# Score copies from PSUM on ScalarE, and row maxima by a reduction on VectorE, in a top-k attention kernel

## The chip, the cores and the metric

The kernel runs on one core of a Trainium2 chip. The metric is the device time of one execution in microseconds: 3460.84 us in the median of three runs, 3460.31 to 3461.46.

## What is computed

For 32 batches of 256 tokens with 256 features: a gated cross attention with 16 heads that keeps the 64 largest scores of a row, then a gated linear layer with operands rounded to an 8-bit float format.

```python
def _topk_attention(Q, K, V, topk):                     # topk = 64, d = 16
    scores = jnp.einsum('bhqd,bhkd->bhqk', Q, K) / jnp.sqrt(jnp.asarray(d, Q.dtype))
    topk_scores, topk_idx = jax.lax.top_k(scores, topk)
    probs = jax.nn.softmax(topk_scores, axis=-1)
    sel = gather(V, topk_idx)
    return jnp.einsum('bhqk,bhqkd->bhqd', probs, sel)

x = x + tanh(g_xattn) * attention(layernorm(x), ctx, ctx)      # projections Wq, Wk, Wv, Wo with biases
x = x + tanh(g_ffn) * fp8_linear(layernorm(x))
```

## The kernel before

The order of every engine is written out by hand, one function for each engine, and semaphores join them. A batch has two **stages**, g = 0 and g = 1, of 8 heads each; stage i = 2b + g. A head has two tiles of 128 query rows by 256 keys (jh = 0, 1), so a stage has 16 score tiles of 128 x 256, and `score_sb` is a ring of four stages. A stage is worked in four **quarters**, r = 0 to 3. While VectorE finishes stage i, four stages are in hand at once:

- Stage i + 2: its scores arrive. PE (`scores`, L615) computes a head into one of the two halves `ps_s[:, n % 2]` of PSUM, each 512 wide, and may go on to head H when H - 1 heads have been copied (`s_copied`). VectorE (`copy_scores`, L966) copies a head in two instructions of 256 elements. They read with a step of 16 elements, since the queries stand in PSUM as (j, t) and in `score_sb` as (t, j), and the same instruction takes the row maximum into `mx`. After the eighth head `start_thresholds` (L977 to L980) makes the first threshold X from the maxima.
- Stage i + 1: its thresholds are searched. In each quarter ScalarE counts 14 tiles against X (`guide_counts`, L796, one ACTIVATE and a read of the accumulator each), VectorE the other two (L988); `update_thresholds` (L1003 to L1041) waits for both and moves X, and its last step (L1021 or L1041) releases the next quarter's counts through `s_thr`.
- Stage i: `final_tiles` masks four tiles a quarter (L1066, L1071) and takes the eight largest of the rest (L1077); `final_thresholds` in the last quarter picks the 64th score. Where a row stays unsure, `settle` at the next stage's first quarter sorts it out.
- Stage i - 1: it is mixed. ScalarE takes the exponentials of a head (`exps`, L806), VectorE masks them (`probs`, L1169), PE transposes them (L626), ScalarE evacuates (`evacuate_probs`, L814), and PE multiplies by the values (L641). Exponentials of head n wait until VectorE has masked head n - 2.

ScalarE's order in a quarter is: counts of the stage ahead, then for heads 2r and 2r + 1 an evacuation (of a head four earlier) and the exponentials. Other work stands between: L775 (projections, behind heads 6 of g = 0 and 0 of g = 1), L766 and L767 (front, behind head 4 of g = 0), L783 (`queries_by_head`, 3.6 us, behind head 5 of g = 1), L821 (mixed values, ahead of heads 0 and 4).

VectorE's order in a quarter is: masks of the finals, two counts, copies of head 2r in two halves around L1071, L1077, masking of one head of probabilities, the update with the masking of a second head and the copies of head 2r + 1 between its steps. In the last quarter the copies of head 2r + 1 and the start of the thresholds stand ahead of the update:

```python
if last and has(1):
    for jh in range(2):
        copy_scores(i + 2, fresh, 2 * r + 1, jh)
    start_thresholds(i + 2, fresh)
steps = update_thresholds(i + 1, ahead, r) if guided else iter(())
```

Ahead of the batches VectorE copies the scores of stages 0 and 1. SP issues the DMAs that turn queries and keys by way of DRAM; GpSimd does layernorms and the splitting of operands. `schedule` writes out four batches at either end and loops over pairs of batches between.

## Time and profile before

| | |
|---|---|
| median of the runs | 3460.84 us |
| the profiled execution: from its first to its last instruction (span) | 3454.8 us |
| VectorE busy | 3099.7 us, 90% |
| ScalarE busy | 2725.2 us, 79% |
| PE busy | 1812.2 us, 52% |
| GpSimd busy | 669.6 us, 19% |
| the chain that ended last | VectorE 54%, ScalarE 18%, issue 18%, PE 6% |

The profile gives no device time of its own for the profiled execution, only its span; the median of the runs lies 6.0 us above it. The chain is followed back from the last instruction, at each step to what released it. "Issue" is time in which an engine waited for nothing that the profile shows. An instruction's row may overlap the next one's on its engine, so the cost of one in a full queue is the distance of the starts.

### The profile page before, as it was taken

The page shows a single profiled execution, that of the slowest core. Times are in us where ns is not written, and L with a number is a line of the kernel's source. Part 1 is how long each engine was busy: PE and PEld are TensorE (multiplying, and loading weights), DVE is VectorE, ACT ScalarE, POOL GpSimd, SP SyncE. Part 2 cuts the span into 40 slices and gives each one's busy share as a digit, 9 for nine tenths or more (in the row PEclk, how much of TensorE's full clock was granted, in tenths as well). Part 3 has the DMA queues.
Part 4 walks back from the last instruction along what each step waited for, and adds up shares of the span by engine and source line. Part 5 has one row for each costly group of instructions (what it writes and reads, how often), then busy time and mean ns, then how long its engine had stood idle before and what let it go on. Part 6 is the DMA issues. An engine that isn't in the chain of part 4 may idle for free.

```text
span 3454.8 us, 50006 instructions
## 1 busy us (share of the span) xinstructions
PE 1812.2 (52%) x6928; PEld 973.4 (28%) x6928; DVE 3099.7 (90%) x13458; ACT 2725.2 (79%) x9158; POOL 669.6 (19%) x914
## 2 busy tenths in 40 slices
PE   4155555555455555455555555555455455554555
PEld 2122232322223323222232233322223222232222
DVE  2798999999999999999989999999999999999995
ACT  3788788878688888787878888788788788887872
POOL 3111121121122121111211212121211112211112
PEclk7577677777777777677777777777677777777767
DMA  5122333322233222332223333222333123332111
GB/s 95 29 32 49 49 53 56 53 40 47 47 49 59 45 44 44 51 53 44 46 43 54 56 52 58 41 42 46 51 57 50 33 45 59 49 59 35 26 23 44
DMA packets 425740, 164.74 MB, mean 48 GB/s; under 512 B 219504, under 2 KB 425328, under 8 KB 425408
## 3 DMA queue, kind: packets, MB, share of 16 engines
q1 hardware_dynamic: 425024, 161.54, 27.4%
q14 instruction: 314, 2.57, 0.3%
q0 software_dynamic: 384, 0.33, 0.1%
q8 instruction: 18, 0.29, 0.0%
HBM read 102.57 MB, written 59.24 MB: 47 GB/s over the span
## 4 chain that ended last, share of the span: by engine, by line
DVE 54%; ACT 18%; issue 18%; PE 6%; DVEq 2%; DMA 1%; POOL 0%; SPq 0%; ACTq 0%; POOLq 0%
ACT act_junk L796 14%; DVE p_sb L1169 8%; DVE masked L1066 6%; DVE masked L1071 5%; DVE score_sb L966 5%; DVE following L1077 4%; DVE dve_junk L988 3%; DVE fbias_sb L1213 2%; DVE A L1013 2%; PE ps_t L626 1%; PE ps_o L641 1%; ACT qs L783 1%; PE ps_a L592 1%; ACT pT_sb L814 1%; DVE X L1021 1%
## 5 line engine op out<-in xcount | busy, mean ns | idle before, releaser
L796 ACT ACTIVATE act_junk<-score_sb,X 128x256 bf16<-128x256 f32 x3584 | 1764.7, 498 | 104.4 <-DVE X L1041 79.1
L626 PE MATMUL ps_t<-ident,p_sb 128*128 128x128 f32 x2048 | 452.7, 362 | 1497.6 <-DVE p_sb L1169 893.8
L806 ACT ACTIVATE e_sb<-score_sb,nmx 128x256 f32<-128x256 f32 x1024 | 466.2, 505 | 516.7 <-DVE p_sb L1169 511.7
L626 PEld LDWEIGHTS ps_t<-ident,p_sb 128*128 128x128 f32 x2048 | 322.3, 187 | 1586.7 <-issue 891.1
L641 PE MATMUL ps_o<-pT_sb,v_aug 128*32 128x256 f32 x2048 | 767.9, 515 | 0.5 <-ACT pT_sb L814 0.5
L796 ACT ACTIVATION_READ_ACCUMULATOR act_junk<-score_sb,X 128x1 f32 x3584 | 684.5, 191 | 0.0
L1169 DVE SCALAR_TENSOR_TENSOR p_sb<-score_sb,thr,e_sb 128x256 f32<-128x256 f32 x1024 | 505.6, 515 | 17.9 <-PE ps_t L626 5.0
L966 DVE TENSOR_SCALAR_CACHE_REDUCE score_sb<-ps_s 128x256 f32<-128x256 f32 x1024 | 416.5, 413 | 50.7 <-PE ps_s L615 50.4
L1066 DVE TENSOR_SCALAR_CACHE_REDUCE masked<-score_sb,X 128x256 f32<-128x256 f32 x1024 | 426.0, 471 | 11.0 <-issue 7.7
L1077 DVE MAX8 following<-masked 128x8 f32<-128x256 f32 x1024 | 357.4, 408 | 1.1 <-DVE masked L1071 0.9
L641 PEld LDWEIGHTS ps_o<-pT_sb,v_aug 128*32 128x32 f32 x2048 | 232.3, 136 | 318.9 <-issue 268.0
L1071 DVE SCALAR_TENSOR_TENSOR masked<-masked,score_sb 128x1024 f32<-128x1024 f32 x256 | 313.3, 1224 | 0.1
L814 ACT COPY pT_sb<-ps_t 128x512 f32<-128x512 f32 x512 | 294.0, 574 | 3.9 <-PE ps_o L641 3.9
L499 POOL CAST split<-proj 128x512 bf16<-128x512 f32 x64 | 42.2, 660 | 1157.6 <-ACT proj L775 980.3
L615 PE MATMUL ps_s<-ks,qs 96*128 96x256 bf16 x1024 | 224.4, 306 | 59.7 <-DVE score_sb L966 45.1
L988 DVE SCALAR_TENSOR_TENSOR dve_junk<-score_sb,X,minus_twos 128x256 bf16<-128x256 f32 x512 | 227.4, 480 | 0.1
L472 POOL TENSOR_SCALAR var<-mv 128x2 f32<-128x2 f32 x64 | 14.2, 222 | 805.4 <-DVE mv L912 802.8
L528 POOL TENSOR_TENSOR ysum_sb<-y_sb,magic_sb 128x512 f32<-128x512 f32 x32 | 44.0, 1374 | 562.1 <-DVE magic_sb L938 562.1
L615 PEld LDWEIGHTS ps_s<-ks,qs 96*128 96x128 bf16 x1024 | 76.6, 103 | 251.3 <-issue 128.2
L783 ACT COPY qs<-q_rows 96x4096 bf16<-96x4096 bf16 x32 | 115.0, 3593 | 12.9 <-DMA q_rows<-q_scr 12.9
L1003 DVE TENSOR_TENSOR X<-aim,count 128x16 f32<-128x16 f32 x256 | 48.1, 188 | 84.9 <-ACT act_junk L796 62.6
L601 PE MATMUL ps_a<-wT,cT 128*128 128x256 f32 x256 | 101.6, 535 | 0.0
(149 smaller groups left out, 3088.0 us busy)
## 6 DMA issues: line engine op xcount, KB each, us to landing
...
o_scr<-o_sb SPq DMA_DIRECT2D x128, 128.0 KB, 2.8
...
```

What stands on the lines that cost most here:

```text
L615: ins = nc.tensor.matmul(ps_s[:, n % 2, jh * TOK:(jh + 1) * TOK], qs[p][:, h, 8 * jh:8 * jh + 8, :].rearrange("d j t -> d (j t)"), ks[p][: ...
L626: ins = nc.tensor.transpose(ps_t[:, n % 2, kc * TOK + jh * P:kc * TOK + jh * P + P], p_sb[:, n % 2, jh, kc * P:kc * P + P], ident[:])
L641: ins = nc.tensor.matmul(ps_o[32 * c:32 * c + 32, half * TOK:(half + 1) * TOK], v_aug[p][:, 2 * h + kc, :], pT_sb[:, n % 2, kc * TOK:(kc + ...
L796: ins = nc.scalar.activation(act_junk[:, t, :], score_sb[:, slot, t, :], ACT.Sign, scale=-1.0, bias=X[slot % 2][:, 0, t:t + 1], accum_out= ...
L806: ins = nc.scalar.activation(e_sb[:, n % 2, jh, :], score_sb[:, slot, t, :], ACT.Exp, bias=nmx[:, slot, t:t + 1])
L814: nc.scalar.copy(pT_sb[:, n % 2, :], ps_t[:, n % 2, :]).then_inc(s_PT, 1)
L966: ins = nc.vector.tensor_scalar(dst, src, 0.0, None, ALU.add, ALU.max, accum_out=mx[:, slot, t:t + 1])
L988: ins = nc.vector.scalar_tensor_tensor(dve_junk[:, t - ACT_TILES, :], score_sb[:, slot, t, :], X[slot % 2][:, 0, t:t + 1], minus_twos[:], ...
L1066: nc.vector.tensor_scalar(masked[:, k, :], score_sb[:, slot, t, :], X[slot % 2][:, 0, t:t + 1], None, ALU.is_gt, ALU.add, accum_out=final_ ...
L1071: nc.vector.scalar_tensor_tensor(masked[:], masked[:], -BIG, scores, ALU.mult, ALU.add).then_inc(s_fin, 1)
L1077: nc.vector.max(following[:, t, 1:], masked[:, k, :]).then_inc(s_fin, 1)
L1169: ins = nc.vector.scalar_tensor_tensor(p_sb[:, n % 2, jh, :], score_sb[:, slot, t, :], thr[:, slot, t:t + 1], e_sb[:, n % 2, jh, :], ALU.i ...
```

## The change

ScalarE copies a head's scores, 128 x 512, from PSUM in one instruction, in the same order of elements. It does so ahead of the evacuation and the exponentials of each of the two heads of a quarter, behind the quarter's counts. The copy waits for the scores, and for the probabilities of the stage whose place in the ring it takes. VectorE takes the maxima of a head with one `tensor_reduce` over 2 x 256 in SBUF; it waits for the copy. Heads 2r and 2r + 1 of a quarter are no longer reduced in the places of their copies: the first quarter has head 0 alone, the next two have two heads each (2r - 1 and 2r), the last has heads 5, 6 and 7. `start_thresholds` waits for the eighth reduction. Ahead of the batches ScalarE makes the 16 copies of stages 0 and 1, behind both calls of `queries_by_head` and ahead of its first counts.

```diff
--- before.py
+++ after.py
@@ -240,6 +240,7 @@
         s_va = sem("values_ready")
         s_S = sem("scores_in_psum")
         s_copied = sem("scores_copied")
+        s_max = sem("maxima_ready")
         s_step = sem("selection_steps")
         s_sel = sem("selected")
         s_exp = sem("exp_done")
@@ -797,6 +798,14 @@
                                                bias=X[slot % 2][:, 0, t:t + 1], accum_out=count[slot % 2][:, t:t + 1])
                 ins.then_inc(s_cnt, 1)
 
+            def copy_scores(i, slot, n):
+
+                H = GH * i + n
+                act.wait_ge(s_S, H + 1)
+                act.wait_ge(s_P, at(H - RING * GH + 1))
+                nc.scalar.copy(score_sb[:, slot, 2 * n:2 * n + 2, :].rearrange("p a (t j) -> p a t j", j=NJ),
+                               ps_s[:, n % 2, :].rearrange("p (a j t) -> p a t j", a=2, t=D)).then_inc(s_copied, 1)
+
             def exps(i, slot, n):
                 H = GH * i + n
                 act.wait_ge(s_sel, i + 1)
@@ -862,6 +871,8 @@
                         if guided:
                             guide_counts(2 * b + g + 1, (2 * p + g + 1) % RING, r)
                         for n in (2 * r, 2 * r + 1):
+                            if has(1):
+                                copy_scores(2 * b + g + 2, (2 * p + g + 2) % RING, n)
                             if mixes:
                                 after_transposes(mb, mp, mg, n, has(-1))
                                 exps(2 * mb + mg, 2 * mp + mg, n)
@@ -880,6 +891,9 @@
                             if has(-3) and (g, n) == (0, 7):
                                 evacuate_ffn(b - 3)
 
+            for i in range(2):
+                for n in range(GH):
+                    copy_scores(i, i, n)
             for r in range(GUIDES):
                 guide_counts(0, 0, r)
             schedule(act, batch)
@@ -955,22 +969,17 @@
             nc.vector.tensor_tensor(kq_sb[:], y_sb[:], magic_sb[:], ALU.add).then_inc(s_kq, 1)
             dve.wait_ge(s_kq, 1)
 
-            def copy_scores(i, slot, n, jh):
-
-                H = GH * i + n
-                if jh == 0:
-                    dve.wait_ge(s_S, H + 1)
-                t = 2 * n + jh
-                src = ps_s[:, n % 2, jh * TOK:(jh + 1) * TOK].rearrange("p (j t) -> p t j", t=D)
-                dst = score_sb[:, slot, t, :].rearrange("p (t j) -> p t j", j=NJ)
-                ins = nc.vector.tensor_scalar(dst, src, 0.0, None, ALU.add, ALU.max, accum_out=mx[:, slot, t:t + 1])
-                if jh == 1:
-                    ins.then_inc(s_copied, 1)
+            def row_maxima(i, slot, n):
+
+                dve.wait_ge(s_copied, GH * i + n + 1)
+                carry(dve)
+                nc.vector.tensor_reduce(mx[:, slot, 2 * n:2 * n + 2], score_sb[:, slot, 2 * n:2 * n + 2, :], AX.X,
+                                        ALU.max).then_inc(s_max, 1)
 
             def start_thresholds(i, slot):
 
                 x = X[slot % 2]
-                dve.wait_ge(s_copied, GH * i + GH)
+                dve.wait_ge(s_max, GH * i + GH)
                 carry(dve)
                 dve.wait_ge(s_thr, at(GUIDES * i))
                 carry(dve)
@@ -1220,8 +1229,7 @@
             front_moments(1)
             for i in range(2):
                 for n in range(GH):
-                    copy_scores(i, i, n, 0)
-                    copy_scores(i, i, n, 1)
+                    row_maxima(i, i, n)
                 if i == 0:
                     start_thresholds(0, 0)
             for r in range(GUIDES):
@@ -1249,13 +1257,11 @@
                             guide_counts(i + 1, ahead, r)
                         if r == 0 and mixes:
                             read_unsure(i - 1)
-                        if has(1):
-                            copy_scores(i + 2, fresh, 2 * r, 0)
                         next(finals)
                         if r == 0 and mixes:
                             convert_unsure(i - 1)
-                        if has(1):
-                            copy_scores(i + 2, fresh, 2 * r, 1)
+                        if has(1) and r:
+                            row_maxima(i + 2, fresh, 2 * r - 1)
                         next(finals, None)
                         if r == 0 and mixes:
                             settle(i - 1, mixed)
@@ -1268,8 +1274,8 @@
                                 probs(of, at_slot, first, jh)
                         last = r == GUIDES - 1
                         if last and has(1):
-                            for jh in range(2):
-                                copy_scores(i + 2, fresh, 2 * r + 1, jh)
+                            for n in (2 * r, 2 * r + 1):
+                                row_maxima(i + 2, fresh, n)
                             start_thresholds(i + 2, fresh)
 
                         steps = update_thresholds(i + 1, ahead, r) if guided else iter(())
@@ -1282,8 +1288,8 @@
                             next(steps, None)
                         for jh in range(2):
                             next(ending, None)
-                            if has(1) and not last:
-                                copy_scores(i + 2, fresh, 2 * r + 1, jh)
+                            if has(1) and not last and jh:
+                                row_maxima(i + 2, fresh, 2 * r)
                             next(steps, None)
                         for _ in ending:
                             next(steps, None)
```

ScalarE from head 5 in the third quarter to the end of the fourth, in a stage g = 1, before. The names are those of the text above; `qs` are the rearranged queries.

```order
L814 COPY pT_sb<-ps_t 128x512
L806 ACTIVATE e_sb<-score_sb,nmx 128x256 x2
L783 COPY qs<-q_rows 96x16x16x16
L796 ACTIVATE act_junk,count<-score_sb,X 128x256 x14
L814 COPY pT_sb<-ps_t 128x512
L806 ACTIVATE e_sb<-score_sb,nmx 128x256 x2
L814 COPY pT_sb<-ps_t 128x512
L806 ACTIVATE e_sb<-score_sb,nmx 128x256 x2
```

The same place in the changed kernel, where L797 are the counts, L806 the new score copy, L815 the exponentials, L823 the evacuation and L784 the queries:

```order
L806 COPY score_sb<-ps_s 128x512
L823 COPY pT_sb<-ps_t 128x512
L815 ACTIVATE e_sb<-score_sb,nmx 128x256 x2
L784 COPY qs<-q_rows 96x16x16x16
L797 ACTIVATE act_junk,count<-score_sb,X 128x256 x14
L806 COPY score_sb<-ps_s 128x512
L823 COPY pT_sb<-ps_t 128x512
L815 ACTIVATE e_sb<-score_sb,nmx 128x256 x2
L806 COPY score_sb<-ps_s 128x512
L823 COPY pT_sb<-ps_t 128x512
L815 ACTIVATE e_sb<-score_sb,nmx 128x256 x2
```

Three copies have come in (that of head 4 stands ahead of this piece, right behind the third quarter's counts), and the last of them, of head 7, stands behind the copy, evacuation and exponentials of head 6.

VectorE in the fourth quarter, before, behind its counts L988 and up to the update L1003:

```order
L966 TENSOR_SCALAR score_sb,mx<-ps_s 128x256
L1071 SCALAR_TENSOR_TENSOR masked<-masked,score_sb 128x1024
L966 TENSOR_SCALAR score_sb,mx<-ps_s 128x256
L1077 MAX following<-masked 128x8 x4
L966 TENSOR_SCALAR score_sb,mx<-ps_s 128x256 x2
L977 TENSOR_SCALAR nmx<-mx 128x16
L978 TENSOR_SCALAR X<-mx 128x16
L979 MEMSET A 128x32
L980 MEMSET B 128x32
L1003 TENSOR_TENSOR X<-aim,count 128x16
```

And in the changed kernel, where L976 is the reduction, L986 to L989 the start of the thresholds and L1012 the update:

```order
L1080 SCALAR_TENSOR_TENSOR masked<-masked,score_sb 128x1024
L976 TENSOR_REDUCE mx<-score_sb 128x2
L1086 MAX following<-masked 128x8 x4
L976 TENSOR_REDUCE mx<-score_sb 128x2 x2
L986 TENSOR_SCALAR nmx<-mx 128x16
L987 TENSOR_SCALAR X<-mx 128x16
L988 MEMSET A 128x32
L989 MEMSET B 128x32
L1012 TENSOR_TENSOR X<-aim,count 128x16
```

Four half-copies have gone, a reduction stands ahead of L1086, and two reductions, of heads 6 and 7, stand where two half-copies stood ahead of the start of the thresholds and the update.

## Rows read from the trace of the kernel before

**Rows 1.** The page, part 1: busy us, share of the span, instructions, by engine.

```profile
PE 1812.2 (52%) x6928; PEld 973.4 (28%) x6928; DVE 3099.7 (90%) x13458; ACT 2725.2 (79%) x9158; POOL 669.6 (19%) x914
```

**Rows 2.** Grouped lines: line, engine, operation, tiles, shapes, count | busy us, mean ns | idle before, releasers.

```profile
L806 ACT ACTIVATE e_sb<-score_sb,nmx 128x256 f32<-128x256 f32 x1024 | 466.2, 505 | 516.7 <-DVE p_sb L1169 511.7 <-DVEq L1161 4.8
...
L966 DVE TENSOR_SCALAR_CACHE_REDUCE score_sb<-ps_s 128x256 f32<-128x256 f32 x1024 | 416.5, 413 | 50.7 <-PE ps_s L615 50.4 <-DVE B L980 0.2
...
L1003 DVE TENSOR_TENSOR X<-aim,count 128x16 f32<-128x16 f32 x256 | 48.1, 188 | 84.9 <-ACT act_junk L796 62.6 <-DVE B L980 21.8 <-issue 0.4
```

**Rows 3.** Timeline of VectorE, stage g = 1: start us, us, instruction [idle before].

```profile
1932.46 0.16 DVE L1003 TENSOR_TENSOR X<-aim,count 128x16 f32<-128x16 f32 x1
...
1955.60 0.41 DVE L966 TENSOR_SCALAR_CACHE_REDUCE score_sb<-ps_s 128x256 f32<-128x256 f32 x1
...
1955.94 0.41 DVE L966 TENSOR_SCALAR_CACHE_REDUCE score_sb<-ps_s 128x256 f32<-128x256 f32 x1
...
1956.71 0.38 DVE L977 TENSOR_SCALAR nmx<-mx 128x16 f32<-128x16 f32 x1 [0.36 <-DVE score_sb L966]
...
1957.61 0.18 DVE L1003 TENSOR_TENSOR X<-aim,count 128x16 f32<-128x16 f32 x1 [0.37 <-DVE B L980]
```

**Rows 4.** Timeline of ScalarE, the same stretch.

```profile
1936.01 0.51 ACT L796 ACTIVATE act_junk<-score_sb,X 128x256 bf16<-128x256 f32 x1 [1.25 <-DVE X L1041]
...
1942.91 0.34 ACT L821 COPY o_sb<-ps_o 128x256 f32<-128x256 f32 x1
...
1949.29 0.51 ACT L796 ACTIVATE act_junk<-score_sb,X 128x256 bf16<-128x256 f32 x1
...
1956.18 0.57 ACT L814 COPY pT_sb<-ps_t 128x512 f32<-128x512 f32 x1
...
1957.45 0.57 ACT L814 COPY pT_sb<-ps_t 128x512 f32<-128x512 f32 x1
```

**Rows 5.** Timelines of VectorE and ScalarE, stage g = 0 of the same batch.

```profile
1985.79 0.16 DVE L1003 TENSOR_TENSOR X<-aim,count 128x16 f32<-128x16 f32 x1
...
1996.15 0.19 ACT L796 ACTIVATION_READ_ACCUMULATOR act_junk<-score_sb,X 128x1 f32 x1
1996.24 0.35 ACT L821 COPY o_sb<-ps_o 128x256 f32<-128x256 f32 x1
...
1996.60 0.18 DVE L1003 TENSOR_TENSOR X<-aim,count 128x16 f32<-128x16 f32 x1 [0.72 <-ACT act_junk L796]
...
2000.47 0.53 ACT L796 ACTIVATE act_junk<-score_sb,X 128x256 bf16<-128x256 f32 x1
...
2007.37 0.58 ACT L814 COPY pT_sb<-ps_t 128x512 f32<-128x512 f32 x1
...
2008.21 0.17 DVE L977 TENSOR_SCALAR nmx<-mx 128x16 f32<-128x16 f32 x1 [0.72 <-DVE score_sb L966]
...
2008.64 0.83 ACT L775 ACTIVATE proj<-ps_a,b_col 128x256 f32<-128x256 f32 x2
2009.35 0.59 ACT L814 COPY pT_sb<-ps_t 128x512 f32<-128x512 f32 x1
...
2008.91 0.18 DVE L1003 TENSOR_TENSOR X<-aim,count 128x16 f32<-128x16 f32 x1 [0.37 <-DVE B L980]
```

**Rows 6.** Grouped lines of the nearest operations.

```profile
L814 ACT COPY pT_sb<-ps_t 128x512 f32<-128x512 f32 x512 | 294.0, 574 | 3.9 <-PE ps_o L641 3.9
...
L821 ACT COPY o_sb<-ps_o 128x256 f32<-128x256 f32 x128 | 44.8, 350 | 14.3 <-PE ps_o L641 14.3
...
L1200 DVE TENSOR_REDUCE rowmax<-yabs_sb 128x2 f32<-128x512 f32 x32 | 21.9, 686 | 1.1
```

**Rows 7.** Timelines of VectorE and ScalarE before the batches begin.

```profile
57.34 0.42 DVE L966 TENSOR_SCALAR_CACHE_REDUCE score_sb<-ps_s 128x256 f32<-128x256 f32 x1 [28.34 <-PE ps_s L615]
...
69.55 3.60 ACT L783 COPY qs<-q_rows 96x4096 bf16<-96x4096 bf16 x1 [12.92 <-DMA q_rows<-q_scr]
...
80.30 0.17 DVE L1003 TENSOR_TENSOR X<-aim,count 128x16 f32<-128x16 f32 x1 [9.14 <-ACT act_junk L796]
```

## The prediction

> **What bounds the kernel now.** I read the page's busy line first: VectorE is busy for 3099.7 us of 3454.8, ScalarE for 2725.2 [rows 1]. VectorE looks like the bound, and a change that takes work from it looks good. The grouped lines correct this. ScalarE's idle time stands almost wholly ahead of the exponentials (516.7 us, of which 511.7 until VectorE's masking of probabilities L1169), and VectorE's update of the thresholds L1003 waits now and then for ScalarE's counts (62.6 us) [rows 2]. So the two engines run in a loop: a threshold X from VectorE starts 14 counts on ScalarE, whose end starts the next update. I therefore take the time from one update (L1003) to another, in two stretches of one batch, and ask in each which engine's own work fills it.
>
> In the stage g = 1, the update of the second quarter starts at 1932.46 and that of the fourth at 1957.61: 25.15 us [rows 3]. ScalarE's rows fill nearly all of it without a wait [rows 4]: X is released 3.55 us after the first of these updates (counts from 1936.01), 14 counts take 6.90 (to 1942.91), the work of heads 4 and 5 and the 3.6 us rearrangement of queries L783 take 6.38 (to 1949.29), the next 14 counts 6.89 (to 1956.18), and the update follows 1.43 later. In the stage g = 0 it is 1985.79 to 2008.91, 23.12 us: 10.45 to the end of the first counts (3.55 and 6.90 again), 4.23, 6.90 and 1.54 [rows 5]. In both, ScalarE is the busy one between the second and the fourth quarter. From a fourth quarter's update to the next second quarter's, VectorE fills the time and ScalarE waits ahead of its exponentials. The two kinds of stretch alternate, and an engine's idle total says nothing about the stretches in which it has none.
>
> **The change part by part.** *What VectorE gives and gets.* A head's two score copies go (starts 0.34 apart, 1955.60 and 1955.94 [rows 3]; so 0.69 a head), and one maximum over 2 x 256 comes. The nearest row is the reduction L1200 over the same 128 x 512, which takes 686 ns [rows 6]; successive rows overlap by 0.07 as the copies' do (413 ns long, 0.34 apart), so 0.62 in a full queue. VectorE's saving is 0.07 us a head, 36 us over 512 heads. Below, a reduction of 1x speed is bounded by 2 x 413 = 826 ns on the one side, and 574 ns (ScalarE's row for 512 elements) on the other; I take 0.69, the same operation on the same shape. The Trainium skill ("VectorE: DVE Perf Modes", section on the TRN2 errata) counts 58 cycles plus one an element from SBUF and 120 from PSUM, at 0.96 GHz. That is an estimate of 594 ns for the reduction and of 392 for each copy, 190 ns saved a head instead of 70; it would take about 0.1 us off each of the 61 exposed reductions below, 6 us in all, and the row decides.
>
> In the first quarter of a stage the two half-copies ahead of the maxima are not replaced there (their head's maximum comes later), which saves 0.69, less 0.07 of overlap that the copy filled. In the second quarter another 0.07 is saved. Where a copy stood between two dependent little steps of the update, two gaps were filled and now one is. A gap is worth something between nothing and the 0.36 that L977 waits for its predecessor [rows 3]; I take 0.13, since L977 also has a second semaphore to pass. Over a first and second quarter that nets to 0.6 us saved a stage, 1.2 a batch, in the stretches where VectorE is the bound. ScalarE's two copies a quarter lie there in its waits ahead of the exponentials.
>
> *What ScalarE gets.* 512 copies of 128 x 512 from PSUM. L814 is such a copy: 574 ns [rows 6], of which 0.10 lies under the next instruction, so 0.48 in the queue (ScalarE's counts overlap by as much: 0.49 apart in rows 4, 6.90 over 14, with an accumulator read behind each). The new one reads PSUM with a step of 16 elements, which no ScalarE row shows; L821 writes in pieces of 16 and takes 350 ns for 256 elements, so 0.70 for 512 is the upper end, 0.57 the lower, and I take 0.57, because VectorE's copies read with just this step and show no price for it. All 512 add 246 us of ScalarE time. In the stretch from second to fourth update none of it is hidden: heads 4 and 5 add 2 x 0.48 = 0.96.
>
> *The new wait.* In the last quarter the maxima of heads 6 **and 7**, and then the start of the next thresholds, stand ahead of the update (order of VectorE, above). Head 7's copy is on ScalarE behind 14 counts, the copy of head 6, the evacuation L814 and the exponentials of head 6, and in g = 0 the evacuation of a projection too (order of ScalarE, above). The update used to wait for the counts alone. From the counts' end: copy 0.48, evacuation and exponentials 1.27 (1956.18 to 1957.45 [rows 4]), copy 0.57, release 0.27 (the counts' last row ends at 1996.34, the update starts at 1996.60 [rows 5]), reduction 0.69, wait for its result 0.42 (0.36 [rows 3] and the queue), start of thresholds 0.70 (2008.21 to 2008.91 [rows 5]; 0.90 in rows 3, where L977 took 0.38): 4.40 in g = 1, and with the projection's 0.71 (2008.64 to 2009.35 [rows 5]) 5.12 in g = 0. Behind this wait on VectorE stand the update, the final thresholds of the stage and the next masks; on ScalarE the exponentials of head 7 wait for those masks, so both engines lose it.
>
> *The sums.* g = 1: 3.61 + 6.90 + (6.38 - 0.08 of a wait that goes + 0.96 = 7.26) + 6.89 + 4.40 = 29.06, against 25.15: +3.91. g = 0: 3.61 + 6.90 + (4.23 + 0.96 = 5.19) + 6.90 + 5.12 = 27.72, against 23.12: +4.60. A batch is +8.5 - 1.2 = +7.3 (3.61 is the 3.55 with 0.06 more for the update: 0.13 of a gap less 0.07 of a reduction). Stages 1 to 61 prepare scores and mix at once, 30.5 batches: +223. Stage 0 has no exponentials on ScalarE: +2.
>
> *Waits for scores.* VectorE waits 50.4 us for PE at its copies, 28.3 of it at the first copy of the program [rows 2, 7]. The other 22 go, because ScalarE comes for those heads only after its counts: -22.
>
> *The prologue.* On ScalarE the first score copies stand behind both rearrangements of queries, and the second of them waits for a DMA until 69.55 and ends at 73.1 [rows 7]. VectorE began copying at 57.34. Now 16 copies follow 73.1. Two heads lie ready; the other 14 go round through PE and two buffers, at no less than ScalarE's 0.48 each and about 0.85 if release, copy and release (0.27, 0.57, 0.27) and PE's part all show; I take 0.75, so until 84.5; counts of 6.9 and the release bring the first update to 91.7 instead of 80.30 [rows 7]: +11.
>
> The sum against the profiled execution is 223 + 2 - 22 + 11 = +214, so a span of 3669. The median of the runs stands 6.0 above that span, so **3675 us**, 6.2% slower.
>
> **The rivals.** *The copies fit into ScalarE's waits* (faster). 246 us of copies against 511.7 us of waiting [rows 2], and PE gets its buffers from an engine that waits anyway. Then VectorE's 0.6 a stage is kept in 61 stages (-37), PE's waits go (-22) and only the prologue is lost (+11): 3413. It decides if head 7's copy has ended when VectorE comes to its maximum, which asks for 2.3 us of slack behind ScalarE's counts in the fourth quarter; the rows show ScalarE going from count to count there. For it speaks only the total. 6%.
>
> *Only the new wait costs* (slower, less). Heads 4 and 5 are copied in time that the rows of other batches leave free: 61 x 0.96 = 59 less, 3616. Against it, L783 and the front evacuations follow without a gap [rows 4, 5]. 8%.
>
> *The strided read is slow on ScalarE* (slower, more). If each of the 16-element steps cost another pass, a copy would take 0.44 us longer. Four copies of a stage stand on the path, 61 x 4 x 0.44 = 107, and the prologue 16 x 0.44 = 7: 3789. VectorE reads the same pattern at 413 ns for 256 elements, which speaks against it. The Trainium skill ("SBUF — State Buffer", on SBUF "cachelines") says that PSUM has lines of 8 bytes and that a non-contiguous access slows matmuls significantly; a step of 64 bytes would be hit by that if it holds for a ScalarE read, and by that rule the time is this rival's. No run here shows it yet. 10%.
>
> *It comes out even* (the prologue and the wait paid by VectorE's savings): nothing in the sums is near; 1%.
>
> **How the numbers follow.** My forecast has 75%; within it the copy may be 0.70 (+31), the reduction 0.62 or 0.83, and the dependent gaps may be absent (-8), so 3620 to 3720. The range takes in the milder rival at 3616 and half of the strided one: 3610 to 3760. A difference of under 0.2% could not be told from none. Faster 0.06, same 0.01, slower 0.93.
>
> **What would show each step.** The copy's row on ScalarE at 0.57 to 0.60 us, the reduction at 0.69. VectorE idle ahead of the reductions until ScalarE's copy, about 3.5 us a stage and some 200 us in all, almost all in fourth quarters. ScalarE's counts in third and fourth quarters start without idle time; its busy time near 2970, VectorE's near 3065. From a second quarter's update to a fourth's: 29.1 in g = 1, 27.7 in g = 0. The first update near 91.7. I am wrong if VectorE's wait at the reductions is under 100 us in all, if the copy takes over 0.7, or if the steps from fourth to second quarter, which should shorten by 0.6, lengthen instead.

## The result, and the profile after

The changed kernel takes 3649.11 us in the median of four runs (3648.31 to 3651.48); the kernel before takes 3460.57 on the same chip. The ratio is 1.0551, with a 95% interval of 1.0538 to 1.0564: slower, inside the predicted range and 26 us under the predicted time.

The page of the changed kernel, its first line of parts 1 and 4, and the grouped lines that answer to rows 1, 2 and 6 (L976 is the reduction, L806 the new copy, L815 the exponentials, L1012 the update):

```profile
PE 1867.2 (51%) x6928; PEld 982.3 (27%) x6928; DVE 3049.9 (84%) x11959; ACT 2967.7 (81%) x9670; POOL 662.9 (18%) x914
...
DVE 38%; ACT 37%; issue 19%; DVEq 2%; PE 2%; DMA 1%; ACTq 1%; POOL 0%; SPq 0%; POOLq 0%
...
L815 ACT ACTIVATE e_sb<-score_sb,nmx 128x256 f32<-128x256 f32 x1024 | 469.0, 511 | 484.5 <-DVE p_sb L1178 480.0
...
L976 DVE TENSOR_REDUCE mx<-score_sb 128x2 f32<-128x512 f32 x512 | 348.2, 682 | 282.9 <-ACT score_sb L806 275.6
...
L806 ACT COPY score_sb<-ps_s 128x512 f32<-128x512 f32 x512 | 294.3, 577 | 3.1 <-PE ps_s L616 3.1
...
L1012 DVE TENSOR_TENSOR X<-aim,count 128x16 f32<-128x16 f32 x256 | 62.9, 246 | 83.5 <-ACT act_junk L797 60.1
```

The copy lasts 577 ns and the reduction 682, as forecast (0.57 and 0.69). VectorE's load fell by 50 us and ScalarE's rose by 243, yet ScalarE's idle time ahead of its exponentials fell by only 32 (516.7 in [rows 2]). That difference hides two larger ones: by the steps from one update to the next, this idle time grew by 121 us in the steps behind a fourth quarter's update (152.8 to 274.2) and fell by 155 in the others. The copies used up idle time in one place, and the new wait made it in another. A wait of 275.6 us is new, ahead of the reductions; 46.1 of it is before the batches, so 229.5 is in the loop. On the chain that ended last ScalarE's share went from 18% to 37%.

VectorE at the end of a fourth quarter of g = 1 (start, us, instruction, idle before it and its releaser; this answers to [rows 3]):

```profile
2077.08 0.69 DVE L976 TENSOR_REDUCE mx<-score_sb 128x2 f32<-128x512 f32 x1 [2.27 <-ACT score_sb L806]
2078.84 0.69 DVE L976 TENSOR_REDUCE mx<-score_sb 128x2 f32<-128x512 f32 x1 [1.08 <-ACT score_sb L806]
2079.87 0.17 DVE L986 TENSOR_SCALAR nmx<-mx 128x16 f32<-128x16 f32 x1 [0.34 <-DVE mx L976]
...
2080.56 0.18 DVE L1012 TENSOR_TENSOR X<-aim,count 128x16 f32<-128x16 f32 x1 [0.37 <-DVE B L989]
```

And ScalarE in the same stretch (to [rows 4]), with the last counts first:

```profile
2075.86 0.51 ACT L797 ACTIVATE act_junk<-score_sb,X 128x256 bf16<-128x256 f32 x1
...
2076.35 0.58 ACT L806 COPY score_sb<-ps_s 128x512 f32<-128x512 f32 x1
2076.82 0.59 ACT L823 COPY pT_sb<-ps_t 128x512 f32<-128x512 f32 x1
2077.29 0.93 ACT L815 ACTIVATE e_sb<-score_sb,nmx 128x256 f32<-128x256 f32 x2
2078.11 0.58 ACT L806 COPY score_sb<-ps_s 128x512 f32<-128x512 f32 x1
```

The row behind the last counts starts at 2076.35, which is taken as the counts' end here as in the prediction, and the update starts at 2080.56, 4.21 us later (4.40 forecast; 1.43 before). In between stands exactly the forecast chain: copy of head 6, evacuation and exponentials, copy of head 7, reduction, start of the thresholds. In g = 0 the two waits are 2.28 and 1.80 and the update starts 5.16 after the counts' end (5.12 forecast), since the projection's evacuation L776 stands there too.

The means of all steps from one update's start to the next, over stages 8 to 58 (us). A column is the quarter whose update ends the step, so the first quarter's step begins at the fourth update of the stage before, and the columns of g = 1 begin behind a stage g = 0. The numbers 1 to 12 are those of the experiments below. The last column is explained under the table.

| kernel | g=1: 1st | 2nd | 3rd | 4th | g=0: 1st | 2nd | 3rd | 4th | batch | overlap |
|---|---|---|---|---|---|---|---|---|---|---|
| before | 15.22 | 12.60 | 11.13 | 14.03 | 14.27 | 13.92 | 11.03 | 12.46 | 104.67 | 149 |
| after | 13.01 | 12.14 | 11.09 | 17.79 | 14.09 | 13.73 | 11.43 | 16.88 | 110.15 | 104 |
| 1 copy7_early | 14.60 | 11.81 | 11.09 | 16.62 | 14.02 | 13.84 | 11.30 | 14.78 | 108.06 | 153 |
| 2 max_behind_update | 16.74 | 12.13 | 11.09 | 13.95 | 16.46 | 14.09 | 11.09 | 12.12 | 107.67 | 122 |
| 3 before_short_splits | 13.60 | 10.71 | 11.14 | 14.01 | 13.79 | 14.18 | 10.86 | 12.35 | 100.65 | 51 |
| 4 after_short_splits | 12.53 | 11.29 | 11.20 | 17.79 | 13.52 | 13.92 | 11.22 | 16.68 | 108.15 | 40 |
| 5 scalar_heads_0_to_3 | 14.50 | 12.48 | 11.78 | 14.05 | 13.86 | 13.92 | 11.38 | 12.28 | 104.25 | 142 |
| 6 scalar_heads_0_to_5 | 14.59 | 12.50 | 11.51 | 14.62 | 13.89 | 13.72 | 11.43 | 12.97 | 105.22 | 138 |
| 7 scalar_heads_0_to_3_and_prologue | 14.66 | 12.36 | 11.96 | 14.11 | 13.74 | 13.64 | 11.51 | 12.55 | 104.55 | 143 |
| 8 before_late_projection | 14.10 | 12.46 | 11.13 | 14.03 | 14.25 | 13.97 | 11.11 | 12.28 | 103.32 | 100 |
| 9 heads_0_to_3_late_projection | 13.87 | 12.52 | 11.78 | 14.04 | 13.86 | 13.72 | 11.59 | 12.17 | 103.56 | 107 |
| 10 after_late_projection | 13.82 | 12.48 | 11.09 | 17.78 | 14.05 | 13.72 | 11.42 | 15.93 | 110.30 | 108 |
| 11 scalar_heads_0_and_1 | 14.69 | 13.00 | 11.16 | 14.05 | 13.88 | 14.63 | 10.86 | 12.58 | 104.83 | 136 |
| 12 before_again | 15.19 | 12.60 | 11.14 | 14.03 | 14.25 | 13.97 | 10.99 | 12.53 | 104.70 | 148 |

From second to fourth update (third and fourth columns together) a batch grew by 3.72 in g = 1 and 4.82 in g = 0; 3.91 and 4.60 were forecast. That part of the prediction holds to 0.2 us. The rest of the batch shrank by 3.04 where 1.2, and 22 us of waits for PE in the whole run (0.7 a batch), were forecast; most of that is in one step, 15.22 to 13.01.

**What shrank there.** VectorE's same instructions do not always take the same time. The last column adds up, over all VectorE rows that are more than 80 ns above the median of their line and operation, what they are above it: 149 us before, 104 after. I call this the overlap: all of these rows lie beside a row of GpSimd. The column counts too little, because two lines stand beside GpSimd's splitting nearly always, so that their median is itself a stretched one. One of them, the last addition of the feed-forward (shortest, median and longest ns):

```profile
L1217 DVE SCALAR_TENSOR_TENSOR x_res<-fbias_sb,tg,x_res x32: 752/1526/1529, 463.1 to 3451.5; 128x512 f32<-128x512 bf16 x32
```

Counted against the rows of the same line that meet no GpSimd row, the overlap is 188 us before and 128 after, and 51 and 40 in the kernels with short splits below. I keep the column for comparisons and name the fuller count where it matters. The timeline of both engines before, at the fourth update of a stage g = 0:

```profile
1805.34 0.61 POOL L499 CAST split<-proj 128x512 bf16<-128x512 f32 x1 [24.15 <-ACT proj L775]
1805.60 0.37 DVE L1003 TENSOR_TENSOR X<-aim,count 128x16 f32<-128x16 f32 x1 [0.37 <-DVE B L980]
1805.90 0.28 DVE L1087 TENSOR_TENSOR place<-final_count,ranks 128x128 f32<-128x128 f32 x1
1806.03 1.16 POOL L501 TENSOR_TENSOR rest<-proj,split 128x512 f32<-128x512 f32 x1
1806.10 1.37 DVE L1169 SCALAR_TENSOR_TENSOR p_sb<-score_sb,thr,e_sb 128x256 f32<-128x256 f32 x1
1807.36 0.61 POOL L504 CAST split<-rest 128x512 bf16<-128x512 f32 x1 [0.17 <-POOL rest L501]
...
1808.05 1.15 POOL L506 TENSOR_TENSOR rest<-rest,split 128x512 f32<-128x512 f32 x1
1808.09 1.14 DVE L1009 SCALAR_TENSOR_TENSOR newton<-X,mx 128x16 f32<-128x16 f32 x1
```

A masking L1169 that takes 515 ns in the mean takes 1.37 us, and an operation on 128 x 16 takes 1.14 instead of 0.17: each ends 0.03 to 0.3 us after the GpSimd row in which it began. The splitting starts because the projection's evacuation L775 has just ended on ScalarE, and so its rows meet the update in this stage. After the change the same place reads:

```profile
2134.07 0.61 POOL L500 CAST split<-proj 128x512 bf16<-128x512 f32 x1 [25.57 <-ACT proj L776]
2134.76 1.15 POOL L502 TENSOR_TENSOR rest<-proj,split 128x512 f32<-128x512 f32 x1
```

```profile
2134.52 0.69 DVE L976 TENSOR_REDUCE mx<-score_sb 128x2 f32<-128x512 f32 x1 [1.80 <-ACT score_sb L806]
...
2136.84 1.37 DVE L1178 SCALAR_TENSOR_TENSOR p_sb<-score_sb,thr,e_sb 128x256 f32<-128x256 f32 x1
...
2138.83 0.16 DVE L1018 SCALAR_TENSOR_TENSOR newton<-X,mx 128x16 f32<-128x16 f32 x1
```

The first two GpSimd rows now lie beside VectorE's new wait and a reduction, which is not stretched (0.69); L1018, the 1.14 of before, is 0.16 (0.18 at most over the run). The stretching has not gone, the masking L1178 still takes 1.37 here, but behind g = 0's fourth update the overlap fell from 92 to 44 us over the run. So some 48 us less of it is paid in that step, the one that shrank most, while GpSimd's first rows lie in VectorE's wait. That the wait is what hides it is put to the test by experiments 1, 3 and 4.

The Trainium skill ("SBUF — State Buffer", section "Who interferes with whom") says that VectorE and GpSimd share a port pair under an exclusive lock; that a VectorE instruction with two inputs in SBUF contends with a GpSimd one that reads SBUF; that some one-input operations do in a mode with both ports; and that a reduction, or a `tensor_scalar` that writes its accumulator, never does. The trace agrees in kind. Among the rows before that lie beside a GpSimd row for at least half their length, 66 of the 122 maskings L1169 are stretched, and none of 207 rows of L1066, 124 MAX8 of L1077 and 32 reductions L1200. What separates the maskings is the row in which they begin. Of 63 that begin while GpSimd casts, adds, subtracts or multiplies large tiles (L499 to L509, L515, L519), with more than 50 ns of that row to go, 62 are stretched; of 27 that begin in L476, on 128 x 2, none is. It also goes the other way round: L483 of GpSimd takes 0.56 us in the median, and 1.51 in the 31 rows that begin while VectorE's mask L1071, with two inputs, is running. Of the 35 rows of L1071 beside GpSimd only 2 are stretched, and of 69 counts L988, which stand mostly beside GpSimd's L479 on 128 x 2, only 2.

### The profile page after: what moved, and what is told of

It is laid out like the page before. It is cut to its first block, busy times and chain, and to the rows that moved or that the text cites. A ratio compares the mean times of both kernels' runs of the same rounds, so it can differ in the third digit from the quotient of the medians.

```text
span 3649.7 us, 50441 instructions
## 1 busy us (share of the span) xinstructions
PE 1867.2 (51%) x6928; PEld 982.3 (27%) x6928; DVE 3049.9 (84%) x11959; ACT 2967.7 (81%) x9670; POOL 662.9 (18%) x914
## 4 chain that ended last, share of the span: by engine, by line
DVE 38%; ACT 37%; issue 19%; DVEq 2%; PE 2%; DMA 1%; ACTq 1%; POOL 0%; SPq 0%; POOLq 0%
ACT act_junk L797 23%; DVE p_sb L1178 6%; DVE masked L1075 4%; ACT e_sb L815 4%; ACT score_sb L806 3%; DVE following L1086 3%; DVE mx L976 2%; ACT qs L784 2%; ACT pT_sb L823 2%; DVE masked L1080 2%; DVE dve_junk L997 2%; DVE fbias_sb L1222 1%; DVE above L1015 1%; DVE masked L1122 1%; DVE X L1012 1%
## 5 line engine op out<-in xcount | busy, mean ns | idle before, releaser
L797 ACT ACTIVATE act_junk<-score_sb,X 128x256 bf16<-128x256 f32 x3584 | 1765.8, 502 | 84.9 <-DVE X L1050 59.8
L627 PE MATMUL ps_t<-ident,p_sb 128*128 128x128 f32 x2048 | 468.3, 372 | 1627.1 <-ACT pT_sb L823 975.5
L815 ACT ACTIVATE e_sb<-score_sb,nmx 128x256 f32<-128x256 f32 x1024 | 469.0, 511 | 484.5 <-DVE p_sb L1178 480.0
L642 PE MATMUL ps_o<-pT_sb,v_aug 128*32 128x256 f32 x2048 | 801.6, 534 | 0.5 <-ACT pT_sb L823 0.5
L797 ACT ACTIVATION_READ_ACCUMULATOR act_junk<-score_sb,X 128x1 f32 x3584 | 700.9, 196 | 0.0
L976 DVE TENSOR_REDUCE mx<-score_sb 128x2 f32<-128x512 f32 x512 | 348.2, 682 | 282.9 <-ACT score_sb L806 275.6
L1178 DVE SCALAR_TENSOR_TENSOR p_sb<-score_sb,thr,e_sb 128x256 f32<-128x256 f32 x1024 | 507.2, 517 | 22.1 <-issue 9.4
L1086 DVE MAX8 following<-masked 128x8 f32<-128x256 f32 x1024 | 357.8, 411 | 6.3 <-DVE masked L1080 0.9
L823 ACT COPY pT_sb<-ps_t 128x512 f32<-128x512 f32 x512 | 302.6, 591 | 3.9 <-PE ps_o L642 3.9
L806 ACT COPY score_sb<-ps_s 128x512 f32<-128x512 f32 x512 | 294.3, 577 | 3.1 <-PE ps_s L616 3.1
L616 PE MATMUL ps_s<-ks,qs 96*128 96x256 bf16 x1024 | 231.9, 316 | 71.6 <-ACT score_sb L806 66.8
L1012 DVE TENSOR_TENSOR X<-aim,count 128x16 f32<-128x16 f32 x256 | 62.9, 246 | 83.5 <-ACT act_junk L797 60.1
L784 ACT COPY qs<-q_rows 96x4096 bf16<-96x4096 bf16 x32 | 115.4, 3606 | 15.5 <-DMA q_rows<-q_scr 15.5
```

The source lines that it names most:

```text
L616: ins = nc.tensor.matmul(ps_s[:, n % 2, jh * TOK:(jh + 1) * TOK], qs[p][:, h, 8 * jh:8 * jh + 8, :].rearrange("d j t -> d (j t)"), ks[p][: ...
L627: ins = nc.tensor.transpose(ps_t[:, n % 2, kc * TOK + jh * P:kc * TOK + jh * P + P], p_sb[:, n % 2, jh, kc * P:kc * P + P], ident[:])
L642: ins = nc.tensor.matmul(ps_o[32 * c:32 * c + 32, half * TOK:(half + 1) * TOK], v_aug[p][:, 2 * h + kc, :], pT_sb[:, n % 2, kc * TOK:(kc + ...
L797: ins = nc.scalar.activation(act_junk[:, t, :], score_sb[:, slot, t, :], ACT.Sign, scale=-1.0, bias=X[slot % 2][:, 0, t:t + 1], accum_out= ...
L806: nc.scalar.copy(score_sb[:, slot, 2 * n:2 * n + 2, :].rearrange("p a (t j) -> p a t j", j=NJ), ps_s[:, n % 2, :].rearrange("p (a j t) -> ...
L815: ins = nc.scalar.activation(e_sb[:, n % 2, jh, :], score_sb[:, slot, t, :], ACT.Exp, bias=nmx[:, slot, t:t + 1])
```

## The experiments

My theory had two parts: the time from second to fourth update is ScalarE's, lengthened by two copies and by the wait for heads 6 and 7; and the new wait hides a part of what GpSimd costs VectorE. Against it stood that the copies cost in themselves, wherever on ScalarE they stand, and that GpSimd's rows are no matter. Ratios are to the kernel before on the same chip; where kernels of different chips are compared in us, the difference is taken from the ratios.

**1. copy7_early.** Head 7's copy directly behind head 6's on ScalarE.

```diff
-                            if has(1):
+                            if has(1) and n < GH - 1:
                                 copy_scores(2 * b + g + 2, (2 * p + g + 2) % RING, n)
+                            if has(1) and n == GH - 2:
+                                copy_scores(2 * b + g + 2, (2 * p + g + 2) % RING, n + 1)
```

> Only ScalarE's order changes against the changed kernel: the copy of head 7 stands right behind the copy of head 6, ahead of the evacuation and the exponentials of head 6. Theory (the update of the fourth quarter waits for head 7's copy, which stands behind head 6's work on ScalarE): the update comes 3.3 us behind the end of the counts in both stages, where it now comes 4.19 (g = 1) and 5.14 (g = 0) behind; 0.9 + 1.9 = 2.8 us a batch over 30.5 batches, so 85 less: 3564, at most 20 more if GpSimd's work comes to lie beside VectorE's again. VectorE's wait at the reductions L976 falls from 275 us to about 190. Rival (ScalarE's mere load, 246 us more of copies, makes the loss, wherever they stand): the same amount of work, so 3649 within 10.

3587.02 us, 1.0377 (1.0360 to 1.0395). VectorE, the same place of a fourth quarter, g = 1 (L978 is the reduction, L1014 the update):

```profile
2040.27 1.28 DVE L978 TENSOR_REDUCE mx<-score_sb 128x2 f32<-128x512 f32 x2 [2.27 <-ACT score_sb L806]
...
2042.59 0.17 DVE L1014 TENSOR_TENSOR X<-aim,count 128x16 f32<-128x16 f32 x1 [0.37 <-DVE B L991]
```

One wait of 2.27 is left of two, and the update comes 3.0 behind the counts in both stages, where 3.3 was forecast. The fourth quarters gave back 3.27 a batch, 100 us, more than the 85 forecast. But only 60 us were gained, 3 us too few for the forecast with its allowance. The table says where the rest went: the overlap went back from 104 to 153, and the first quarter of g = 1 from 13.01 to 14.60, which is 48 us. The wait that was removed had been hiding GpSimd's work.

**2. max_behind_update.** The reductions of heads 6 and 7 and the start of the thresholds behind the last step of the update.

```diff
-                        if last and has(1):
-                            for n in (2 * r, 2 * r + 1):
-                                row_maxima(i + 2, fresh, n)
-                            start_thresholds(i + 2, fresh)
...
                         for _ in steps:
                             pass
+                        if last and has(1):
+                            for n in (2 * r, 2 * r + 1):
+                                row_maxima(i + 2, fresh, n)
+                            start_thresholds(i + 2, fresh)
```

> Only VectorE's order changes against the changed kernel: in the last quarter the reductions of heads 6 and 7 and the start of the next thresholds stand behind the update and the final thresholds, not ahead of them. Theory (the loss of the fourth quarter is the wait of the update): the update comes 0.4 us behind the counts, the stretch from second to fourth update falls from 28.9 to 25.1 in g = 1 and from 28.3 to 23.5 in g = 0. Given back in part: the next first quarter grows by 1.5 to 2.6 us, because the two reductions and the start (2.3 us) now lie in VectorE's own stretch and ScalarE's counts of that quarter are released later. Net 4.6 us a batch, 140 less: 3510, between 3470 and 3550. VectorE's wait at L976 falls below 80 us, 46 of it in the prologue. Rival (load alone): 3649 within 10.

3579.92 us, 1.0356 (1.0339 to 1.0374): a miss, 70 us over. The grouped lines:

```profile
L797 ACT ACTIVATE act_junk<-score_sb,X 128x256 bf16<-128x256 f32 x3584 | 1766.6, 502 | 275.3 <-DVE X L987 219.2 <-DVE X L1050 52.6 <-DVE X L1030 3.4
...
L976 DVE TENSOR_REDUCE mx<-score_sb 128x2 f32<-128x512 f32 x512 | 342.5, 681 | 72.0 <-ACT score_sb L806 45.2 <-DVE X L1050 19.5 <-DVE B L989 0.3
...
L1012 DVE TENSOR_TENSOR X<-aim,count 128x16 f32<-128x16 f32 x256 | 49.3, 192 | 209.0 <-ACT act_junk L797 208.6 <-issue 0.4
```

The fourth quarter behaved: 25.04 and 23.21 from second to fourth, the wait for copies in the loop gone. But the threshold X that L987 starts is what the next stage's first counts need, and it now comes last. ScalarE waits 219.2 us for it, and VectorE's next update then waits 208.6 for the counts: the first quarters grew by 3.73 and 2.37 where at most 2.6 was forecast. A good part of the price is paid one quarter later: 67 us were gained where 140 were forecast. The start of the thresholds has to be early and the maxima of heads 6 and 7 are late; neither of the two orders heals that, and others on VectorE were not tried.

**3 and 4. before_short_splits, after_short_splits.** GpSimd's four lower split operations on 16 columns instead of the whole width, in both kernels; left out are the middle and low parts of queries and keys beyond those columns. The first of the four lines (the others are cut likewise, and the tiles are set to zero once at the start):

```diff
-                    nc.gpsimd.tensor_tensor(rest[:], proj[k][:], hi, ALU.subtract).then_inc(s_sp, 1)
+                    nc.gpsimd.tensor_tensor(rest[:, :, 0:16], proj[k][:, :, 0:16], hi[:, :, 0:16], ALU.subtract).then_inc(s_sp, 1)
```

> The kernel before, with GpSimd's splitting of operands cut short: four of the five operations of each split work on 16 columns of 256, so the two lower levels of queries and keys are zero in the rest, and the scores carry the rounding of the first level alone. VectorE, ScalarE and PE have the same instructions. In the trace of before, VectorE's rows exceed the median of their kind by 149 us in sum, and all of that is in rows that overlap a GpSimd row; in the changed kernel it is 104 us. Theory (work of GpSimd that runs beside VectorE makes VectorE's instructions longer, and the change moved 45 us of that into VectorE's wait): this kernel is 100 to 140 faster than before, 3320 to 3360. Rival (the overlap is a coincidence, the rows are long for another reason): 3460 within 10, apart from 11 us for each tile of rows that is sorted out more or less.

> The changed kernel with the same shortened splits on GpSimd (the two lower levels of queries and keys left out beyond 16 columns). Theory: only 60 to 95 faster than the changed kernel, 3555 to 3590, since 45 of the 149 us had gone already; so the distance between the two kernels with short splits is about 234 us instead of 189. Rival: 3649 within 10, distance 189.

3356.46 us, 0.9712 (0.9696 to 0.9728), and 3588.43 us, 1.0378 (1.0361 to 1.0395). Both lie inside their ranges, at the upper ends. VectorE's maskings in the two kernels before, with whole and with short splits (same work, same count):

```profile
L1169 DVE SCALAR_TENSOR_TENSOR p_sb<-score_sb,thr,e_sb 128x256 f32<-128x256 f32 x1024 | 505.6, 515 | 17.9 <-PE ps_t L626 5.0 <-issue 4.6 <-DVE score_sb L1117 3.8
```

```profile
L1171 DVE SCALAR_TENSOR_TENSOR p_sb<-score_sb,thr,e_sb 128x256 f32<-128x256 f32 x1024 | 487.2, 497 | 17.8 <-PE ps_t L628 5.8 <-issue 5.5 <-DVE score_sb L1119 4.2
```

The time fell by 101 us, although both kernels sort two tiles of rows more than the trace of before does (nine and not seven, 22 us; sorted tiles are explained at experiment 12), since the scores differ. By the fuller count the overlap fell by 137 us, from 188 to 51. So before the change most of what GpSimd cost VectorE stood in the open. After the change the same cut gives 60 (1.0551 to 1.0378), with one tile more, where the fuller count fell by 88. With short splits the change costs 232 us and not 189, and a batch grows by 7.50, where the prediction, which counted no overlap, had 7.3. What the short splits leave open is whether an earlier end of GpSimd's work helps in other ways too; VectorE's waits for PE did not fall by it.

**5. scalar_heads_0_to_3.** ScalarE copies heads 0 to 3 alone (first and second quarter, where it has waits); heads 4 to 7 and the copies ahead of the batches stay on VectorE as they were.

```diff
-                            if has(1):
+                            if has(1) and n < GH // 2:
                                 copy_scores(2 * b + g + 2, (2 * p + g + 2) % RING, n)
...
+                        if has(1) and r == 2:
+                            row_maxima(i + 2, fresh, 3)
+                        if has(1) and r >= 2:
+                            copy_half(i + 2, fresh, 2 * r, 0)
```

> ScalarE copies heads 0 to 3 only (first and second quarter) and VectorE reduces them; heads 4 to 7 are copied by VectorE in two halves with the maxima taken in the same instruction, as before, and so are the 16 heads ahead of the batches. Theory (ScalarE is the bound from the second to the fourth update and VectorE elsewhere, and the loss is ScalarE's copies there and the wait for head 7): the stretch from second to fourth update is that of before, 25.1 and 23.5 us; the other stretch is 0.6 shorter a stage. 61 stages: 37 less than before, 3424 against a before of 3460; 3410 to 3440. GpSimd's overlap stays as before (149 us of excess). Rival (the reduction on VectorE and the double handling cost by themselves, wherever they stand): half of the loss of the changed kernel stays, about 3555. One tile of rows was sorted out more in every kernel with ScalarE's copies so far (8 instead of 7, 11 us each); if it comes from the values that ScalarE copies, it may or may not be here, by the head it is in.

3455.79 us, 1.0003 (0.9994 to 1.0012) in 11 runs: a miss. The added wait is gone and so are 187 of the 189 us, but no gain is left in the time. The first quarters gained 0.72 and 0.41, and with the second ones 1.25 a batch, which is what the prediction of the change had for these two quarters (1.2). The third of g = 1 lost 0.65, that of g = 0 0.35: head 3's reduction stands at its head. A batch is 0.42 shorter in all, 13 us, and one more sorted tile (experiment 12) takes 11 of them.

VectorE in this third quarter of g = 1, with the reduction L985, the half-copies L977 and the maskings L1189:

```profile
1943.19 0.68 DVE L985 TENSOR_REDUCE mx<-score_sb 128x2 f32<-128x512 f32 x1
1943.79 0.41 DVE L977 TENSOR_SCALAR_CACHE_REDUCE score_sb<-ps_s 128x256 f32<-128x256 f32 x1
...
1946.93 0.86 DVE L1189 SCALAR_TENSOR_TENSOR p_sb<-score_sb,thr,e_sb 128x256 f32<-128x256 f32 x2
```

And ScalarE in the same kernel and place:

```profile
1947.82 0.51 ACT L815 ACTIVATE e_sb<-score_sb,nmx 128x256 f32<-128x256 f32 x1 [0.56 <-DVE p_sb L1189]
```

I had counted the reduction's 0.69 as free, since ScalarE is the bound of that stretch. It delays the maskings behind it, and the exponentials, which stand ahead of the fourth quarter's counts, now wait 0.56 for them. The stretch from second to fourth update of g = 1 grew by 0.67.

**6. scalar_heads_0_to_5.** Only heads 6 and 7 stay on VectorE; against kernel 5:

```diff
-                            if has(1) and n < GH // 2:
+                            if has(1) and n < 6:
...
-                        if has(1) and r == 2:
-                            row_maxima(i + 2, fresh, 3)
                         if has(1) and r >= 2:
+                            row_maxima(i + 2, fresh, 2 * r - 1)
+                        if has(1) and r == 3:
```

> The same with heads 0 to 5 on ScalarE, and heads 6 and 7 on VectorE. Against the kernel with heads 0 to 3 this puts two copies of 0.48 us on ScalarE's stretch between second and fourth update and takes nothing from VectorE's. Theory: 61 x 0.96 = 59 more than with heads 0 to 3, about 3483, so a little slower than before; no wait at the reductions. The remaining step to the changed kernel (3649), 165 us, is the wait for head 7 and the prologue. Rival (ScalarE has room for the copies of the third quarter): the same as with heads 0 to 3.

3485.60 us, 1.0091 (1.0077 to 1.0105). The time was forecast at 3483, and that it came so near is luck: the forecast stood on 3424 for kernel 5, 32 us too low, and on a step of 59 from there, 29 too high. The steps say more. Two copies behind the third quarter's counts bring 26.13 and 24.40 from second to fourth update, which is before's 25.16 and 23.49 with 0.97 and 0.91 more, the forecast 2 x 0.48. Against kernel 5, though, it is 30 us more and not 59: kernel 5 had already paid in its third quarter. The step from this kernel to the whole change is 159 us: the price of moving heads 6 and 7 (and of the copies ahead of the batches).

**7. scalar_heads_0_to_3_and_prologue.** Kernel 5 with the 16 copies ahead of the batches on ScalarE.

```diff
+            for i in range(2):
+                for n in range(GH):
+                    copy_scores(i, i, n)
             for r in range(GUIDES):
                 guide_counts(0, 0, r)
```

> Heads 0 to 3 on ScalarE in the batches, and all 16 heads ahead of the batches too, behind both rearrangements of queries, as in the changed kernel. Theory: the first update comes at 91 us instead of 80.3, and the whole is 11 us slower than with the prologue's copies on VectorE. Rival (the prologue's delay is caught up, since PE and the DMAs were behind there anyway): within 3 us.

3470.31 us, 1.0047 (1.0033 to 1.0061): 15 more than kernel 5 where 11 was forecast. The first update came at 91.0 instead of 81.2.

**8, 9 and 10. before_late_projection, heads_0_to_3_late_projection, after_late_projection.** The kernel before, kernel 5 and the changed kernel, with the evacuation of the first projection moved behind head 7, so that GpSimd's splitting starts later, not under the fourth update.

```diff
-                            if has(2) and (g, n) == (0, 6):
-                                evacuate_projection(b + 2, 0)
...
+                            if has(2) and (g, n) == (0, 7):
+                                evacuate_projection(b + 2, 0)
```

> The kernel before with one piece of ScalarE's order moved: the evacuation of the query projection L775, which releases GpSimd's split, stands behind the exponentials of head 7 (and the evacuation of the feed-forward) instead of behind those of head 6. Theory (GpSimd's split beside VectorE's update makes VectorE's two-input and fast instructions wait, 92 of the 149 us of excess in the quarter between the g = 0 stage's last update and the next): the split now lies beside VectorE's masks, copies and MAX8, none of which was ever long beside a GpSimd row. The excess of that quarter falls from 92 to 20 to 40 us, and the kernel is 50 to 70 faster than before: 3385 to 3405. Rival (the length of those rows is not GpSimd's doing): the same time within 7.

> The kernel with heads 0 to 3 copied by ScalarE, with the same move of L775. Theory: the same 50 to 70 faster than without it, so 3385 to 3405, and within 10 of the kernel before with the move; VectorE's 0.07 us a head is too little to show. It holds one tile more to sort out (11 us).

> The changed kernel with the same move. Theory: L775's 0.71 us is no longer ahead of head 7's copy in g = 0, so the fourth quarter's update there comes 4.4 us behind the counts instead of 5.14: 22 less in 31 batches. GpSimd's split no longer lies in VectorE's wait but beside its masks: excess of 104 us within 20 of what it was. 3610 to 3640. Rival (the excess comes back in full once the split leaves the wait): 3649 or more.

3431.07 us, 0.9938 (0.9924 to 0.9951); 3432.26 us, 0.9941 (0.9927 to 0.9955); 3630.84 us, 1.0509 (1.0493 to 1.0525). The first is the fastest kernel with whole splits, but a miss, and so is the second: 22 us were won where 50 to 70 were forecast. Behind this update the overlap fell from 92 to 49 us, not to 20 to 40. The loop gives 1.35 a batch, 41 us, of which the sorted tile takes 11. The splitting has moved but still meets VectorE's work. Both engines in before_late_projection at the same place:

```profile
1798.51 0.18 DVE L1003 TENSOR_TENSOR X<-aim,count 128x16 f32<-128x16 f32 x1 [0.37 <-DVE B L980]
1798.83 0.48 DVE L1169 SCALAR_TENSOR_TENSOR p_sb<-score_sb,thr,e_sb 128x256 f32<-128x256 f32 x1
1799.97 0.48 DVE L1169 SCALAR_TENSOR_TENSOR p_sb<-score_sb,thr,e_sb 128x256 f32<-128x256 f32 x1
```

```profile
1802.86 0.61 POOL L499 CAST split<-proj 128x512 bf16<-128x512 f32 x1 [28.08 <-ACT proj L775]
1803.55 1.15 POOL L501 TENSOR_TENSOR rest<-proj,split 128x512 f32<-128x512 f32 x1
```

The update and its maskings are now at their plain 0.18 and 0.48, and the splitting starts 4.35 us behind the update, not 0.26 ahead. Once this is done the copies of heads 0 to 3 bring nothing more (0.9941 against 0.9938). In the changed kernel the edit takes the projection's evacuation out of the wait for head 7: the fourth quarter of g = 0 falls from 16.88 to 15.93, the forecast 0.7 and a little more, but 0.81 comes back in the first quarter (13.01 to 13.82) and 0.34 in the second, so that a batch is no shorter. The median, 3630.84, lies in the forecast range all the same. The execution that was profiled was the slowest of its five, at 3651.6, so its trace shows these steps but not where the median's 15 us went.

**11. scalar_heads_0_and_1.** Only the first quarter's heads go to ScalarE; against kernel 5:

```diff
-                            if has(1) and n < GH // 2:
+                            if has(1) and n < 2:
...
-                        if has(1) and r == 2:
-                            row_maxima(i + 2, fresh, 3)
-                        if has(1) and r >= 2:
+                        if has(1) and r == 1:
+                            row_maxima(i + 2, fresh, 1)
+                        if has(1) and r >= 1:
```

> ScalarE copies heads 0 and 1 only. For the time: as with heads 0 to 3, the same as before within 10. For the tile that is sorted out more in all five kernels with ScalarE's copies of heads 0 to 3 in the batches (behind the 20th update, in batch 2), and in none without: if the values of ScalarE's copy differ from VectorE's in some element of heads 2 or 3, the extra tile goes (56 rows of MAX8 L1111 instead of 64); if it is in heads 0 or 1, or comes from something else that these kernels share, it stays.

3474.35 us, 1.0058 (1.0042 to 1.0073), 21 us over the kernel before where 10 at most were expected: a miss. The first quarters gained (14.69, 13.88), and the second ones lost 0.40 and 0.71, a reduction more beside their own four half-copies. A reduction is put off from the quarter of its copy to the next, and the next pays.

**12. before_again.** The kernel before without an edit, as a control.

> The kernel before, unchanged, for one look at its trace in a later run. The extra tile that is sorted out behind the 20th update stands in every kernel profiled since the first trace, also in the one with the late projection, in which VectorE makes all copies; so it is not the values of ScalarE's copies. If it is here too (64 rows of MAX8 L1111), it belongs to the run or the chip and not to the order of a kernel, and 11 us of the distance between the two first traces have nothing to do with the change. If it is not (56 rows), it comes with some shift of timing, and what shifts it stays open. The time is that of before within 0.2%.

3470.58 us, 1.0034 (1.0020 to 1.0048), for the same code. Its trace shows a difference in the data's path: `settle` runs when a row of a tile stays unsure and then sorts the tile with eight MAX8. In the trace of before, and in this one:

```profile
L1111 DVE MAX8 max<-masked 128x8 f32<-128x256 f32 x56 | 24.0, 428 | 1.9
```

```profile
L1111 DVE MAX8 max<-masked 128x8 f32<-128x256 f32 x64 | 27.4, 428 | 2.2
```

Seven tiles against eight, each about 11 us. The changed kernel and every one of mine with whole splits have the same eight; the two with short splits have nine. Outside that tile the control's loop is that of before: 104.70 a batch against 104.67. So one tile's 11 us in each difference to "before" is not the change's, and neither ScalarE's copy nor the reduction makes it, as I had first thought. Why the same code takes the branch once more often in one set of runs is open. Kernels of mine compare with each other untouched; against the control the change costs 1.0551 / 1.0034, about 1.052, kernel 5 stands at 0.997, a gain of some 11 us, and before_late_projection at 0.990.

## Why the prediction was right, point by point

- **What bounds the kernel.** Right. The loop of update and counts, read stretch by stretch, gave the stretch from second to fourth update to 0.2 us in both stages; the engines' totals pointed the other way. Kernels 5 and 6 confirm it from the other side: with heads 6 and 7 on VectorE the 4 us disappear.
- **What VectorE gets.** Copy and reduction cost what their nearest rows cost: the reduction took 682 ns, near its row's 686 and not the 594 of the prediction's other estimate. Kernel 5 has the changed kernel's order in the first and second quarters but not the new wait, and gains 1.25 a batch there, where the prediction had 1.2 and a part of PE's waits; with short splits the changed kernel gains 1.03. A postponed reduction costs in the quarter where it lands (kernels 5 and 11).
- **What ScalarE gets.** 577 ns, the lower end. The strided read has no price, so that rival falls. The Trainium skill ("SBUF — State Buffer", on SBUF "cachelines") says that a non-contiguous access to PSUM significantly slows matmuls; for a ScalarE read with a step of 64 bytes this trace shows nothing of the kind (577 ns beside 574). The 0.96 of heads 4 and 5 was measured by kernel 6 as 0.97 and 0.91.
- **The new wait.** 4.19 and 5.14 in the mean against 4.40 and 5.12. Kernel 2 shows that it is a dependency and not only an order: put behind the update, it returns in good part as a wait for X.
- **The sums.** Second to fourth update 8.54 a batch (8.51 forecast), 260 us over 30.5 batches. The other steps gave back 3.04 a batch, 93 us, where 1.2 a batch and 22 us of PE waits (59) were forecast. This part of the sum was mis-sized, and twice. It had no term for GpSimd: rows of VectorE beside GpSimd's are longer, and a wait can lie there instead. Kernel 5 gives 1.25 of the 3.04 without the new wait; the other 1.8, 55 us, comes with the wait, and with short splits it is gone. And the 22 us were counted in full, though 10 of them lay in the fourth quarters of g = 0, in the stretch that ScalarE fills.
- **The prologue.** The first update at 91.1 (91.7 forecast), 10.8 later than before; kernel 7 gives 9.8 on its own.
- **What was not in the sum.** One more sorted tile, 11 us. The pieces are 167 for the batches (5.48 x 30.5), 10.8 ahead of them and 11: 189, against a difference of the spans of 194.9. The 6 that are left lie between the first and the last update, whose distance grew by 184.2 us; behind the last update both kernels take 103. Where between them is open.
- **Mechanism and luck.** The mechanism that carries the sum, ScalarE's stretch with two more copies and the wait for head 7, is shown. That the whole came within 26 us is in part luck: the hidden overlap made the change some 50 us cheaper than its bare cost of 232, the PE waits were counted too high, and a sorted tile that the change does not make added 11.
- **The rivals.** "The copies fit in ScalarE's waits" falls; the fourth quarters grew by 3.8 and 4.4 us, and the idle time ahead of the exponentials fell by 32 of 512. "Only the new wait costs" falls with kernel 6. "It comes out even" falls with the result.
